# A four-layer graph network on one core: edge messages summed by plain fp32 matmuls with the edge weight in the one-hot

## The reference

```python
def _rgcn_conv(x, src, dst, etype, W, root, b):
    x_src = x[src]
    seg = dst * num_rel + etype
    sums = segment_sum(x_src, seg)
    cnt = segment_sum(ones, seg)
    mean = sums / maximum(cnt, 1.0)[:, None]
    mean = mean.reshape(num_nodes, num_rel, -1)
    out = einsum('nri,rio->no', mean, W)
    return out + x @ root + b
```

## Time and profile before

| | |
|---|---|
| time, median of 3 runs | 2577.93 us (2574.44 to 2586.51) |
| the profiled execution: span from the first to the last instruction | 2573.7 us; its own time is one of the runs above, the nearest of which is 2574.44 us |
| PE busy | 2049.9 us (80%) |
| DVE, ACT, POOL busy | 1448.0 us, 932.1 us, 848.5 us |
| first stretch of messages | 394 to 530 us |
| second stretch | 947 to 1082 us |
| third stretch | 1735 to 1881 us |
| share of the chain that ended last, DMA arena<-U,ixb | 5% |
| mean clock granted to TensorE | 0.839 of full |

### The profile page before, as it was taken

One profiled execution on the slowest core, in us unless ns is written; L12 is line 12 of the kernel. 1 busy time (PEld: TensorE's weight loads), 2 busy tenths in 40 slices (PEclk: granted clock), 3 DMA queues, 4 the chain that ended last, 5 costly groups with the idle time before them and its releaser, 6 DMA issues.

```text
span 2573.7 us, 36363 instructions
## 1 busy us (share of the span) xinstructions
PE 2049.9 (80%) x10546; PEld 1800.4 (70%) x10547; DVE 1448.0 (56%) x2262; ACT 932.1 (36%) x1151; POOL 848.5 (33%) x731
## 2 busy tenths in 40 slices
PE   3999887689998786579999999857688576577775
PEld 3999885468887574379999998844475566547665
DVE  5841227753333367745555554436654799457995
ACT  1222225522222135425454544435530255113443
POOL 0001766710007637512222222017700065002554
PEclk9999898879998798879999999967788756785555
DMA  3556556724444247537877777657720121001111
GB/s 106 160 171 189 143 160 206 238 95 143 143 150 140 76 149 237 184 126 249 263 260 264 263 252 248 224 180 244 222 71 0 48 62 70 28 6 58 62 54 43
DMA packets 206660, 384.96 MB, mean 150 GB/s; under 512 B 19347, under 2 KB 174373, under 8 KB 206590
## 3 DMA queue, kind: packets, MB, share of 16 engines
q1 hardware_dynamic: 173934, 253.16, 30.2%
q0 software_dynamic: 31216, 128.89, 16.9%
q10 hardware_dynamic: 1440, 1.97, 0.2%
HBM read 295.56 MB, written 88.39 MB: 149 GB/s over the span
## 4 chain that ended last, share of the span: by engine, by line
PE 44%; issue 21%; POOL 11%; DVE 10%; DMA 9%; ACT 3%; POOLq 0%; another core or an unknown queue 0%; ACTq 0%; DVEq 0%; SPq 0%
PE ps L1602 34%; POOL arena L570 5%; DMA arena<-U,ixb 5%; POOL counts L497 3%; DMA arena<-in_L_gnn_W_rel 2%; POOL arena L481 2%; PE ps L1615 1%; ACT hT_hi L704 1%; DVE hT_lo L1001 1%; PE ps L1510 1%; PE ps L1728 1%; PE ps L1496 1%; PE ps L1494 1%; PE ps L1455 1%; DVE counts L933 1%
## 5 line engine op out<-in xcount | busy, mean ns | idle before, releaser
L1602 PE MATMUL ps<-w_hi,hT_hi 128*128 128x384 f32 x2172 | 772.6, 356 | 66.0 <-DVE hT_lo L1048 22.1
L1602 PE MATMUL ps<-w_lo,hT_hi 128*128 128x384 f32 x2172 | 744.8, 343 | 1.8 <-issue 1.6
L1602 PE MATMUL ps<-w_hi,hT_lo 128*128 128x384 f32 x2172 | 743.7, 342 | 1.4 <-issue 1.2
L1602 PEld LDWEIGHTS ps<-w_hi,hT_hi 128*128 128x128 f32 x2172 | 422.7, 195 | 80.0 <-issue 51.7
L1602 PEld LDWEIGHTS ps<-w_lo,hT_hi 128*128 128x128 f32 x2172 | 422.8, 195 | 4.6 <-issue 4.3
L1602 PEld LDWEIGHTS ps<-w_hi,hT_lo 128*128 128x128 f32 x2172 | 421.3, 194 | 2.2 <-issue 2.2
L570 POOL TENSOR_TENSOR arena<-arena,counts 128x640 f32<-128x640 f32 x103 | 204.7, 1999 | 470.0 <-DVE arena L1325 470.0
L481 POOL DMA_INDIRECT arena<-U,ixb x252 | 298.6, 1185 | 101.6 <-issue 61.5
L1001 DVE SCALAR_TENSOR_TENSOR hT_lo<-arena,wgt,hT_hi 128x768 fp32r<-128x768 f32 x252 | 256.7, 1019 | 116.2 <-ACT hT_hi L704 95.4
L704 ACT ACTIVATE hT_hi<-arena,wgt 128x768 fp32r<-128x768 f32 x252 | 235.0, 936 | 187.8 <-DMA arena<-U,ixb 161.6
L1769 PE MATMUL ps<-R,arena 128*128 (+2 forms) x1000 | 226.5, 410 | 84.3 <-ACT arena L787 84.1
(11 more groups left out here) (231 smaller groups left out, 2444.3 us busy)
## 6 DMA issues: line engine op xcount, KB each, us to landing
arena<-in_L_gnn_W_rel SPq DMA_DIRECT2D x74, 1152.0 KB, 5.8
U<-arena SPq DMA_DIRECT2D x292, 192.0 KB
arena<-in_L_gnn_W SPq DMA_DIRECT2D x36, 1152.0 KB
U<-z SPq DMA_DIRECT2D x28, 864.0 KB
arena<-terms_d SPq DMA_DIRECT2D x42, 320.0 KB, 3.7
arena<-rows_d SPq DMA_DIRECT2D x21, 320.0 KB, 3.6
arena<-in_L_gnn_root SPq DMA_DIRECT2D x4, 1152.0 KB
arena<-U,ixb POOLq DMA_INDIRECT x252
```

The source lines that it names most:

```text
L1602: ins = pe.matmul(acc, l, r[:, j, kt, :], start=(n == 0), stop=(n == 3 * KT - 1))
```

## The change

For each tile, ACT's and DVE's halves msg_hi and msg_lo are no longer made: ACT's loops of messages go away altogether. DVE makes one instruction, onehot = (iota == place) * wgt, in fp32 instead of fp32r. PE multiplies that one-hot by the gathered rows themselves, in fp32, as two matmuls (512 and 256 columns) in the place of four. PE now waits for the gather's arrival (g_in) and for the one-hot (msg_oh). A gather buffer is freed by PE's end of the tile (agg_pe, raised by GB = 6 at the start instead of MB = 4) and no longer by DVE; DVE's wait is shifted by GB - MB, so that it still runs up to four tiles ahead of PE.

```diff
@@ -74,9 +74,7 @@
         mx_scr = [arena[:, o:o + NP] for o in (7040, 9600, 10240)]
         hrow = arena[0:2 * NG, 10880:10880 + 2 * P].rearrange("p (b n) -> p b n", b=2)
 
-        msg_hi, msg_lo = (t[:].rearrange("p k n -> p (k n)")[:, 0:MB * D].rearrange("p (b n) -> p b n", b=MB)
-                          for t in (hT_hi, hT_lo))
-        onehot = sb("onehot", [P, MB, P], F32R)
+        onehot = sb("onehot", [P, MB, P])
         counts = sb("counts", [P, 2, NG, NP])
         C = counts[:, 0]
         CT = counts[:, 1]
@@ -198,7 +196,7 @@
 
         S = {n: sem(n) for n in (
             "x_in edges_in dve_nop w64_in consts vec_ok ln_var ln_std ln_h hT_tp hT_hi hT_lo "
-            "w_hi w_lo steps evac pool_idx pool_nop msg_hi msg_lo agg_pe acc_out "
+            "w_hi w_lo steps evac pool_idx pool_nop msg_oh agg_pe acc_out "
             "srt_rs srt_ps srt_rhs srt_mm srt_tab cnt_oh cnt_pe k_inv kinv_st w_pr w_done "
             "key_ok key_tp ov_ok urow_st urow_ok u_zero l_oh l_pe l_ix h_st lix_ok hc_tp hc_hi hc_lo "
             "v_in v_hi v_lo v_mm v_ev "
@@ -473,7 +471,7 @@
                 t = j + GU * it
                 b = j % GB
                 table = (0, 0, 3)[phase]
-                pool.wait_ge(S["msg_lo"], NT * phase + t + 1)
+                pool.wait_ge(S["agg_pe"], NT * phase + t + 1)
                 if b == 0:
                     indices(table, it, j, (1, 3, 4)[phase])
                 else:
@@ -694,16 +692,6 @@
                 each_further(act, n_ov, tile)
                 split(0, Q_GCN)
 
-            def messages(ph):
-
-                with act.Fori(0, NT // GU) as it:
-                    for o in range(GU):
-                        t = o + GU * it
-                        act.wait_ge(g_in[o % GB], 16 * (NT // GB * ph + 2 * it + o // GB + 1))
-                        act.wait_ge(S["agg_pe"], NT * ph + t + 1)
-                        act.activation(msg_hi[:, o % MB, :], gat[:, o % GB, :], cp,
-                                       scale=wgt[:, ph // 2, ds(t, 1)]).then_inc(S["msg_hi"], 1)
-
             act.wait_ge(S["consts"], 14)
             act.sem_inc(S["evac"], 2)
             for j in range(2):
@@ -712,16 +700,12 @@
             split(0, 0)
             transpose(0, rl)
             phase(Q_C1, R0, ST_C1)
-            act.wait_ge(S["w_done"], NT // GB + 2)
-            messages(0)
             transpose(1, rl)
             phase(Q_C2, R0, ST_C2)
-            messages(1)
             ln(1)
             transpose(2, rl)
             relations(Q_L1, ST_L1)
             further()
-            messages(2)
 
             for s in range(NG):
                 act.wait_ge(S["ct_tp"], s + 1)
@@ -995,11 +979,9 @@
                     for o in range(GU):
                         t = o + GU * it
                         b = o % MB
-                        dve.wait_ge(S["agg_pe"], NT * ph + t + 1)
-                        dve.tensor_scalar(onehot[:, b, :], iota[:, 1:P + 1], tab[:, 1, ds(t, 1)], None, ALU.is_equal)
-                        dve.wait_ge(S["msg_hi"], NT * ph + t + 1)
-                        dve.scalar_tensor_tensor(msg_lo[:, b, :], gat[:, o % GB, :], wgt[:, ph // 2, ds(t, 1)],
-                                                 msg_hi[:, b, :].bitcast(F32), ALU.mult, ALU.subtract).then_inc(S["msg_lo"], 1)
+                        dve.wait_ge(S["agg_pe"], NT * ph + t + 1 + GB - MB)
+                        dve.tensor_scalar(onehot[:, b, :], iota[:, 1:P + 1], tab[:, 1, ds(t, 1)], wgt[:, ph // 2, ds(t, 1)],
+                                          ALU.is_equal, ALU.mult).then_inc(S["msg_oh"], 1)
 
             def sources():
 
@@ -1180,7 +1162,7 @@
 
             def sums_out(ph, into_x):
 
-                dve.wait_ge(S["agg_pe"], NT * (ph + 1) + MB)
+                dve.wait_ge(S["agg_pe"], NT * (ph + 1) + GB)
                 for c0, c1 in ((0, 512), (512, D)):
                     ins = dve.tensor_tensor((R if into_x else h)[:, :, c0:c1], R[:, :, c0:c1], sums(c0), ALU.add)
                 if into_x:
@@ -1190,7 +1172,6 @@
 
             dve.wait_ge(S["consts"], 14)
             dve.sem_inc(S["w_lo"], 2)
-            dve.sem_inc(S["msg_lo"], GB)
             dve.sem_inc(S["w_done"], 2)
             dve.sem_inc(S["hc_lo"], 1)
             dve.sem_inc(S["v_lo"], 2)
@@ -1504,11 +1485,11 @@
                     for o in range(GU):
                         b = o % MB
                         g = group(it, GU, o)
-                        pe.wait_ge(S["msg_lo"], NT * ph + o + GU * it + 1 + GB)
-                        for part in (msg_hi, msg_lo):
-                            for c0, c1 in ((0, 512), (512, D)):
-                                ins = pe.matmul(sums(c0, g), onehot[:, b, :], part[:, b, c0:c1], start=False,
-                                                stop=part is msg_lo, skip_group_check=True)
+                        pe.wait_ge(S["msg_oh"], NT * ph + o + GU * it + 1)
+                        pe.wait_ge(g_in[o % GB], 16 * (NT // GB * ph + 2 * it + o // GB + 1))
+                        for c0, c1 in ((0, 512), (512, D)):
+                            ins = pe.matmul(sums(c0, g), onehot[:, b, :], gat[:, o % GB, c0:c1], start=False,
+                                            stop=True, skip_group_check=True)
                         ins.then_inc(S["agg_pe"], 1)
 
             def sort(beside):
@@ -1674,7 +1655,7 @@
             pe.sem_inc(S["hc_tp"], 6)
             pe.sem_inc(S["steps"], 10)
             pe.sem_inc(S["c_pe"], 2)
-            pe.sem_inc(S["agg_pe"], MB)
+            pe.sem_inc(S["agg_pe"], GB)
             pe.wait_ge(S["consts"], 14)
             pe.wait_ge(S["ln_h"], NG)
             transpose(0)
```

## The result

| | |
|---|---|
| kernel before, beside the changed one | 2582.22 us (2574.44 to 2590.82, 4 runs) |
| changed kernel | 2542.2 us (2539.79 to 2547.09, 4 runs) |
| ratio | 0.986, 95% interval 0.9825 to 0.9895 |
| profiled execution of the changed kernel | 2542.5 us, span 2540.7 us |

The change makes the kernel 1.4% faster, 40 us of the 70 that were forecast. (The two profiled runs differ by 33.0 us, since the profiled run of the kernel before was the fastest of its four.) The experiments ran on five chips, and what the change is worth differs between them: 2.3% on one (0.9766, interval 0.9724 to 0.9808). I take the result's chip first, since the prediction's steps are set against its trace.

A forecast was written before the change was run, and what follows sets the result against it. POOL's gathers, held by DVE's two-tensor instruction, set the pace of the message stretches. Gains of 64.6 and 5.8 us made -70.4 us: 2507.5 us against the median 2577.93; 8-in-10 range 2488 to 2553 us.

The forecast's parts named there:

- Step 1: Three message stretches: without L1001 on DVE, POOL's gathers run undisturbed, 105.9 us a stretch; gain 64.6 us together.
- Step 3: PE's message products: two fp32 matmuls replace four fp32r, 1.29 us a tile at full clock, under POOL's 1.38 us.
- step 6: Gather buffers: PE frees them after 6.3 us, six buffers allow 8.3 us, so no new wait for POOL.
- Rival C: PE's 0.33 us dispatch exposed: whole 2570 us, half 2532 us; half shares chance 0.20, whole shares 0.11.
- Rivals A: PE's clock in the stretches: halved, 2800 us, chance 0.07; milder dips to 0.9, 2525 us, sharing chance 0.20.
- B: POOL's gathers not freed, full transfer queue makes them long: only 6 us gained, 2572 us; shares chance 0.11.
- D: The change does not do what it says in the message loops; excluded by instruction order, no size or chance given.
- Step 4: DVE's one-hot in the message tiles: stays near 0.28 us, costs gathers below 4 us, taken as nothing.
- Step 5: Way from a stretch's last gather to DVE's sums: 8.25 us becomes about 6.3 us; gain 5.8 us over three.
- Step 7: Gather transfers in the stretches: 285 GB/s needed against 226 to 229 before, costs nothing.

The follow-up runs named there:

- chip A: Chip of the first experiments, kernel before 2542.16 us; less work for PE there: changed kernel without each tile's second product (256 columns), 2477.78 us, one run.
- chip D: Chip where the kernel before was profiled again unchanged, 2575.18 us in one run, beside the changed kernel, 2527.82 us.
- chip C: Chip where the changed kernel ran unedited against the kernel before (2542.99 us): 2484.47 us, ratio 0.9766; with twelve gather buffers 2471.38 us, 0.9717.

## Why the prediction was right and wrong

The time lies inside the range and the sign is right, but the gain was 40 us, not 70.

- **Step 1, POOL is freed, was right in kind and wrong in what it was worth.** Gathers fell to 967 ns (960 forecast), and POOL's own pace is 105.8 us in the first stretch on chip A once PE has less to do (108.1 and 108.8 in the others). Its 105.9 us a stretch did not come on the result's chip: 29.4 us gained instead of 64.6. Its reason was too narrow as well: DVE's one-source instruction holds a gather too. Its count of the gathers holds by the exact records (100 of 170 begun under L1001 are long, none of the 52 begun under nothing). And 132.5 us for the third stretch before was one run; on chip D it is 127.3.
- **The steps that failed are 3 and 6, which put the waits between PE and POOL at nothing.** Step 3 let PE's 1.29 us stand under POOL's 1.38 with 0.09 us to spare, and step 6 said that "no wait comes in its place". On the result's chip a tile takes 1.52 us: POOL stands 1.9 to 2.5 us six times in the first stretch, which is 10.2 of the 11.3 us missing there, and PE 10.6 us in 19 places. By PE's ends the buffers were free in time, as step 6 worked out; the start that should follow came late. On chip C, where it comes in 0.20 us, the same kernel takes 107.2, 108.6 and 110.2 us and gains 58.5 us of the 70.4. So the terms are right for one kind of chip, and on the other 0.09 us to spare was too little; what delays the starts there stays open.
- **Step 3's 1.29 us is right, and a break costs more than its idle time.** Fp32 matmuls of 512 columns start 0.43 us apart at full clock, those of 256 start 0.22 us apart. Behind a wait the first starts its successor after 0.53 us (445.03 and 445.56), 0.10 us more, and the last one's modelled end lies 0.16 us beyond where the next could have started. By estimate each break thus costs 0.26 us beyond the idle time in the rows, 5 us for the 19 of the first stretch.
- **The trace of before had a sign of it,** PE's 26.4 us of waits for issue between the stages, and the prediction did not read it: it asked who waits for whom, and never who waits for nobody.
- **Rival C, half exposed, came nearest in its time,** by luck: 1.45 us a tile and 2532 us, against 1.52 and 2542. Its mechanism is not what happened: the dispatch is hidden behind running matmuls (chip C). Rivals A, B and D are out by the clock, the gathers' mean and the trace.
- **Step 4:** the one-hot grew to 356 ns and holds no gather; PE waits for it 7.6 us in all, of which 5.0 are at the heads of the stretches.
- **Step 5:** 5.8 us forecast, and 5.9 came, by luck: DVE's sums follow the last gather by 7.9, 7.2 and 6.5 us, not 6.3, but before it was 8.25, 10.2 and 9.1 and I had looked at one.
- **Step 6 on chip C:** POOL's idle time is put down to PE before 45 gathers of the first stretch, which hides in its own 0.30 us. Doubling the buffers gave 0.5% there.
- **Step 7:** right; 274 to 279 GB/s flow on chip C, and nothing waits for more.
- The rest of the program moved by +2.3 us (-33.0 us of span, less 29.4 and 5.9): nothing was lost elsewhere, as assumed.

## What to carry to other kernels

When a change lifts a slow engine off the path, list what the next one does in that stretch and beyond it. A margin of 0.09 us in 1.38 held on one chip and failed on three others. Where a profile says that an engine waits for another, look up in the rows when that other was done: here it had been for over a microsecond. Run the unchanged baseline on the same chip as every edit; here an edit that does nothing looked like the whole answer for want of it. The version to keep where it can be had is twelve gather buffers (0.972 of the time before on chip C, against 0.977), but on chips of the slower kind the two versions with more buffers gained nothing from the first product to the sums.

## What was new about the hardware

- Chips (or sessions on them) differ by 1.1 to 1.9% on the same kernel (2542 to 2547 against 2575 to 2590 us). The marks of the slower kind: PE's waits without a cause, 15.6 to 31.5 us against 0.6 in one stage of some 400 us; DVE's starts up to 2.9 us (the result's chip) behind what they wait for, against 0.20; and traces that hold only a part of the gathers' semaphore updates, 1972 of 4032 on the result's chip.
- A gather ends 0.81 to 0.85 us after the DVE instruction that held it at its start, whether that reads one or two SBUF tensors of 768 columns, in 99 cases of 99 in the two runs on it. One source also holds it near its end: ten gathers end 0.12 or 0.13 us after it. Two sources did not, in 52 cases. A one-hot of 128 columns with two per-partition scalars (0.36 us) holds nothing.
- A plain fp32 matmul of 512 columns starts its successor 0.43 us later at full clock; four of them, the tile's 768 columns in two instructions each, are 1.29 us, and 0.10 us more where the array was idle before.
